# One gate before the last matrix product instead of a gate per chunk, and moved waits on the first casts of the q, k, v weights

## The chip, the cores and the metric

The kernel runs on the 8 cores of one Trainium2 chip, the same program on each. The metric is device time in microseconds (us) of the slowest core; lower is better. Each core has TensorE (PE, matrix products), VectorE (DVE), ScalarE (ACT), GpSimd (POOL) and SyncE (SP, here only a queue of transfers). Engines run their own instruction streams, in order, and wait for one another on semaphores.

## The reference, cut to what matters

One layer of a network on x of shape (4, 2048, 2048): a layer norm, linear attention with decay and rotary (16 heads of 128), a residual; a second layer norm, then a gated feed-forward part with a Walsh-Hadamard transform of the hidden vector, and a residual.

```python
    up_gate = jnp.einsum('bsd,hd->bsh', x, W1)        # h = 8192
    up_lin  = jnp.einsum('bsd,hd->bsh', x, W3)
    hidden  = jax.nn.silu(up_gate) * up_lin
    hidden  = fwht(hidden)                            # over all 8192 entries, / sqrt(8192)
    out     = jnp.einsum('bsh,dh->bsd', hidden, W2)
# fwht: h = 1, 2, 4, ..., 4096:  (a, b) -> (a + b, a - b) for entries h apart
...
    x = x + _L0_attn_ref(_layernorm(x), Wq, Wk, Wv, Wo, rms_w)
    x = x + _L0_ffn_ref(_layernorm(x), W1, W2, W3)
```

## The kernel before

Each core takes one half (T = 1024 tokens) of one of the four batch entries and does the whole layer for it, without talking to another core. Activations are kept as features on the 128 partitions by tokens along the free axis: x is 16 blocks of 128 by 1024.

The program is written as one list of instructions per engine, filled by `p.emit(engine, function, waits, inc)`; an engine runs its list in the order in which the Python code emits it. For DVE, ACT and POOL each instruction also waits for the one before it on its own engine and increments that engine's semaphore (`realize`). A wait that is already implied by an earlier wait of the same engine on the same semaphore is not emitted. `p.dma("sp", ...)` puts a transfer on SP's queue, `p.dma("act", ...)` on ACT's, `p.dma("pool", ...)` on POOL's; line 183 is the call that issues them.

The stages, in order of time: the state that the other half of the sequence hands over (L341 to L459); the first layer norm (`emit_layernorm`, L501 to L545, tag ln1), whose DVE part is 16 pairs of a subtraction (L543) and a product (L545) that writes `actA`; the q, k, v projections (L576 to L606); attention per head (L640 to L730); the RMS norm and the Wo product (L833, L843); the second layer norm; the feed-forward part.

**Projections.** For each of 48 weight slabs `gi`, SP loads a slab of 1 MB into `wland`, DVE casts it to bf16 in `wbf` (L587), PE does 32 products of 128x128 by 128x512 into `psumP` (L594), and ACT copies the result out (L603). Two buffers of each take turns. The cast waits for its load, for `ln1_done` (the last DVE instruction of the layer norm) and for the products that read the same buffer two slabs earlier.

**Hidden stage.** For 64 chunks of 128 hidden features, in bit-reversed order: 32 products with W1 (L926), 32 with W3 (L938), SiLU on ACT (L948), the product of the two on DVE (L951), one 128-point Hadamard step as a product with `H128s` (L957), and a copy into `hid` on ACT (L964). The other six levels of the transform join whole chunks: a butterfly on chunks (a, b) is a `tensor_add` (L973) and a `tensor_sub` (L976) on DVE, each 128x1024 bf16, written to free slots of `hid`. `fwht_schedule` emits after each chunk every butterfly that has become possible. After the last chunk, number 63, 63 butterflies are left, 126 DVE instructions. The first 31 finish the five lower levels of the odd chunks; the last 32 are the last level, on (0, 1), (2, 3), ..., (62, 63) in this order.

**Output stage.** out = W2 times hidden, in 4 blocks (`mblk`) of 512 output features. A block sums over all 64 chunks, in 16 groups of 4 chunks. For each group SP loads two halves of 512 KB of W2 into `land1`, ACT casts both into `wb1` (L1029), and PE does 32 products (L1045) into the four accumulators `p8`, which fill PSUM. There are two `wb1` and two `land1` buffers. At the end of a block DVE adds the residual that POOL loaded into `xpb` (L1060), and ACT's queue stores the four results, one after another; the casts of the next block stand behind these stores in ACT's list. The order of the groups, `cg_order`, is sorted by the number of the DVE instruction that finishes the group (`group_ready`), and each chunk's first product waits for the instruction that finished that chunk (`cgate`). Sorting leaves the groups in natural order 0, 1, ..., 15: by the schedule, groups 0 to 15 are finished by butterflies whose counts rise from 162 to 192 in steps of two.

Of the kernel before, what the change touches and what calls it, by code (L numbers as in the profile page):

```python
# [213 lines left out]
def build_program(taps=(), use_collective=True, upto="all"):  # L214
# [115 lines left out]
    for k in range(16):  # L330
        par = k % 2
# [246 lines left out]
    for widx, (wt, dst) in enumerate(((wq_h, q_hbm), (wk_h, k_hbm), (wv_h, v_hbm))):  # L578
        for m in range(16):
            gi = widx * 16 + m  # L580
            par = gi % 2
            p.dma("sp", wland[par][:, :], wt.ap()[m],
                  waits=[("dve", cast_val.get(gi - 2, p05_dve_end)),
                         ("pe", p05_pe_end if gi < 2 else 0),
                         ("act", s7_done if gi < 2 else 0)], inc=f"d_w{par}")
            cast_val[gi] = p.emit(
                "dve", lambda e, par=par: e.tensor_copy(wbf[par][:, :], wland[par][:, :]),  # L587
                waits=[(f"d_w{par}", 16 * (gi // 2 + 1)), ("dve", ln1_done),
                       ("pe", pe_proj.get(gi - 2, 0))], inc="dve")
            mm_waits = [("dve", cast_val[gi]), ("act", evac_val.get(gi - 2, 0))]  # L590
            pe_val = None
            for k in range(16):
                for half in range(2):
                    pe_val = p.emit("pe", lambda e, par=par, k=k, half=half: e.matmul(  # L594
                        psumP[par][:, half * 512:(half + 1) * 512],
                        wbf[par][:, k * 128:(k + 1) * 128],
                        actA[:, k * T + half * 512: k * T + (half + 1) * 512],
                        start=(k == 0), stop=(k == 15)),
                        waits=(mm_waits if (k == 0 and half == 0) else ()),
                        inc=("pe" if (k == 15 and half == 1) else None))  # L600
            pe_proj[gi] = pe_val
            evac_val[gi] = p.emit(
                "act", lambda e, par=par: e.activation(out=stg[par][:, :], in_=psumP[par][:, :],  # L603
                                                       func=AF.Copy),
                waits=[("pe", pe_val), (f"d_s{par}", 16 * store_val.get(gi - 2, 0))], inc="act")
            sv = p.dma("act", dst.ap()[m], stg[par][:, :], inc=f"d_s{par}")  # L606
            store_val[gi] = sv // 16
# [391 lines left out]
    blk_dve = {}  # L999
    p8_pe_val = {}  # L1000
    xb_pref = {}
    def group_ready(cg):
        vals = []
        for c in range(cg * 4, cg * 4 + 4):
            kind, val = chunk_src[c]
            vals.append(val if kind == "dve" else 0)
        return max(vals)
    cg_order = sorted(range(16), key=group_ready)
    for mblk in range(4):
        for m4 in range(4):  # L1010
            mchunk = mblk * 4 + m4
            p.dma("pool", xpb[m4][:, :], xp_hbm.ap()[mchunk],
                  waits=[("d_xp", 16 * xp_dma[15]),
                         ("pe", sa_pe_val[63] if mblk == 0 else 0),
                         ("dve", mul_val[63] if mblk == 0 else 0),
                         ("d_out", 16 * out_dma_val.get((mblk - 1, m4), 0))],
                  inc=f"d_xb{m4}")
            xb_pref[(mblk, m4)] = p.v(f"d_xb{m4}")
        for cgi in range(16):
            cg = cg_order[cgi]  # L1020
            par = cgi % 2
            gi = mblk * 16 + cgi
            for half in range(2):
                p.dma("sp", land1[half][:, :].rearrange("p (c m) -> p c m", c=2),
                      w2_h.ap()[mblk, cg * 4 + 2 * half: cg * 4 + 2 * half + 2].transpose([1, 0, 2]),
                      waits=[("act", w2cast.get((gi - 1, half), cast1_val[(63, half)] if gi == 0 else 0))],
                      inc=f"d_f1{half}")
            for half in range(2):
                w2cast[(gi, half)] = p.emit("act", lambda e, par=par, half=half: e.activation(  # L1029
                    out=wb1[par][:, half * 1024:(half + 1) * 1024], in_=land1[half][:, :],  # L1030
                    func=AF.Copy, scale=W2SCALE),
                    waits=[(f"d_f1{half}", 16 * (64 + gi + 1)),
                           ("pe", p8_pe_val.get(gi - 2, w13_pe_val[62 + par]))], inc="act")
            for cc in range(4):
                c = cg * 4 + cc
                hs = slot_of[c]
                ck, cv = chunk_src[c]
                cgate = cv if ck == "dve" else 0
                for m4 in range(4):
                    for half in range(2):  # L1040
                        st_ = (cgi == 0 and cc == 0)
                        sp_ = (cgi == 15 and cc == 3)
                        p8_pe_val[gi] = p.emit(
                            "pe", lambda e, par=par, cc=cc, m4=m4, half=half, hs=hs,
                                  st_=st_, sp_=sp_: e.matmul(  # L1045
                                p8[m4][:, half * 512:(half + 1) * 512],
                                wb1[par][:, cc * 512 + m4 * 128: cc * 512 + (m4 + 1) * 128],
                                hid[:, hs * T + half * 512: hs * T + (half + 1) * 512],
                                start=st_, stop=sp_),
                            waits=(([("act", w2cast[(gi, 1)])]  # L1050
                                    if (cc == 0 and m4 == 0 and half == 0) else []) +
                                   ([("dve", cgate)] if (m4 == 0 and half == 0) else []) +
                                   ([("dve", evac8.get((mblk - 1, m4), 0))]
                                    if (cc == 0 and half == 0 and cgi == 0) else [])),
                            inc=("pe" if (cc == 3 and m4 == 3 and half == 1) else None))
        blk_pe = p.v("pe")
        for m4 in range(4):
            mchunk = mblk * 4 + m4
            par = m4 % 2
            ev = p.emit("dve", lambda e, m4=m4: e.tensor_add(  # L1060
                xpb[m4][:, :], xpb[m4][:, :], p8[m4][:, :]),
                waits=[("pe", blk_pe), (f"d_xb{m4}", xb_pref[(mblk, m4)])], inc="dve")
            evac8[(mblk, m4)] = ev
            dv = p.dma("act", out_h.ap().rearrange("(k p) t -> p k t", p=128)[:, mchunk, :],
                       xpb[m4][:, :], waits=[("dve", ev)], inc="d_out")
            out_dma_val[(mblk, m4)] = dv // 16
        blk_dve[mblk] = p.v("dve")
# [49 lines left out]
```

How the kernel before makes its waits and increments, by code:

```python
            def f(e):  # L191
                selfsem = plan.sems.get(stream) if stream in plan.STRICT else None
                self_idx = 0
                for (waits, fn, sem, amt, is_self) in plan.ops[stream]:
                    for (s, v) in waits:
                        e.wait_ge(s, v)
                    if is_self and self_idx > 0:
                        e.wait_ge(selfsem, self_idx)
                    inst = fn(e)
                    if sem is not None:
                        inst.then_inc(sem, amt)
                    if is_self:
                        self_idx += 1
```

## Time and profile before

| what | us |
|---|---|
| time, median of 3 runs (range 3819.74 to 4116.42) | 3824.39 |
| the profiled execution, its own time | 3820.43 |
| its span on the slowest core, core 7 | 3818.8 |
| PE busy | 2571.3 (67%) |
| ACT busy | 1012.3 (27%) |
| DVE busy | 971.2 (25%) |

The span runs from the first to the last instruction on the core. A row of the profile's costliest groups reads: source line, engine and operation, output <- inputs, shape, count, then busy time, mean duration, and the idle time of that engine just ahead of it with what ended it. Durations of products overlap on PE (a product of 379 ns is followed by the next after some 216 ns), so busy time counts overlapped stretches once. PEclk is the clock that TensorE was granted, as a share of 2.4 GHz; 0.50 is the lower level, 1.2 GHz.

### The profile page before, as it was taken

The page shows a single profiled execution, that of the slowest core. Times are in us where ns is not written, and L with a number is a line of the kernel's source. Part 1 is how long each engine was busy: PE and PEld are TensorE (multiplying, and loading weights), DVE is VectorE, ACT ScalarE, POOL GpSimd, SP SyncE. Part 2 cuts the span into 40 slices and gives each one's busy share as a digit, 9 for nine tenths or more (in the row PEclk, how much of TensorE's full clock was granted, in tenths as well). Part 3 has the DMA queues.
Part 4 walks back from the last instruction along what each step waited for, and adds up shares of the span by engine and source line. Part 5 has one row for each costly group of instructions (what it writes and reads, how often), then busy time and mean ns, then how long its engine had stood idle before and what let it go on. Part 6 is the DMA issues. An engine that isn't in the chain of part 4 may idle for free.

```text
span 3818.8 us, 33708 instructions; the slowest of 8 cores (3802.6 to 3818.8 us)
## 1 busy us (share of the span) xinstructions
PE 2571.3 (67%) x11196; PEld 1088.7 (29%) x11196; DVE 971.2 (25%) x1312; ACT 1012.3 (27%) x1594; POOL 8.8 (0%) x20
## 2 busy tenths in 40 slices
PE   3355565576998222235478488788588788489888
PEld 0022222213443111111132133333233333134333
DVE  0412112114112444443320412221521221710000
ACT  1112122120111444431201233333233333123222
POOL 0000000000000000000000000000000000000000
PEclk9676776778999555557699699999799999799899
DMA  5422112113554011101141233333233343245453
GB/s 167 121 77 67 50 61 67 33 44 132 193 190 144 33 34 39 36 28 55 57 151 56 69 130 132 113 131 132 87 129 127 118 130 104 83 155 170 162 168 132
DMA packets 124218, 392.51 MB, mean 103 GB/s; under 512 B 12432, under 2 KB 12688, under 8 KB 115600
## 3 DMA queue, kind: packets, MB, share of 16 engines
q1 hardware_dynamic: 107920, 348.41, 27.5%
q10 hardware_dynamic: 13824, 33.56, 2.5%
q0 software_dynamic: 2304, 8.39, 0.7%
q8 instruction: 92, 1.51, 0.2%
q14 instruction: 78, 0.64, 0.1%
HBM read 356.76 MB, written 33.55 MB: 102 GB/s over the span
## 4 chain that ended last, share of the span: by engine, by line
PE 64%; DVE 17%; ACT 8%; issue 6%; DMA 4%; DVEq 1%; ACTq 1%; SPq 0%
PE p L1045 11%; PE pg L926 11%; PE pl L938 11%; PE psumP L594 9%; PE ppj L419 7%; PE psumW L833 3%; DVE htmp L951 2%; DVE hid L976 2%; DVE hid L973 2%; PE p_sx_ln L505 1%; PE p_sx_ln L511 1%; ACT ktp L452 1%; ACT ktil L694 1%; DVE actA L545 1%; DVE scrA L543 1%
## 5 line engine op out<-in xcount | busy, mean ns | idle before, releaser
L1045 PE MATMUL p<-hid,wb 128*128 128x512 bf16 x2048 | 451.5, 384 | 100.9 <-DVE hid L976 52.7
L926 PE MATMUL pg<-actA,wb 128*128 128x512 bf16 x2048 | 459.1, 383 | 43.0 <-DVE actA L545 43.0
L938 PE MATMUL pl<-actA,wb 128*128 128x512 bf16 x2048 | 452.5, 379 | 0.0
L594 PE MATMUL psumP<-actA,wbf 128*128 128x512 bf16 x1536 | 333.8, 381 | 44.4 <-DVE wbf L587 44.4
L419 PE MATMUL ppj<-xlnp,wbfp 128*128 128x512 bf16 x1024 | 259.5, 418 | 81.2 <-DVE wbfp L413 60.1
L1045 PEld LDWEIGHTS p<-hid,wb 128*128 128x128 bf16 x2048 | 201.9, 99 | 350.5 <-issue 115.2
L926 PEld LDWEIGHTS pg<-actA,wb 128*128 128x128 bf16 x2048 | 201.8, 99 | 292.2 <-issue 55.0
L938 PEld LDWEIGHTS pl<-actA,wb 128*128 128x128 bf16 x2048 | 200.4, 98 | 241.6
L951 DVE TENSOR_TENSOR htmp<-gsil,pl 128x1024 bf16<-128x1024 bf16 x64 | 78.1, 1221 | 745.4 <-PE pl L938 745.1
L1029 ACT ACTIVATE wb<-land 128x1024 bf16<-128x1024 f32 x128 | 135.2, 1056 | 404.6 <-PE p L1045 279.9
L964 ACT ACTIVATE hid<-pg 128x1024 bf16<-128x1024 f32 x64 | 65.5, 1024 | 580.5 <-PE pg L957 580.5
L594 PEld LDWEIGHTS psumP<-actA,wbf 128*128 128x128 bf16 x1536 | 150.7, 98 | 228.5 <-issue 48.7
L833 PE MATMUL psumW<-actA,wbf 128*128 128x512 bf16 x512 | 128.6, 415 | 86.7 <-DVE wbf L827 86.7
L705 PE MATMUL tp_O<-stil,vtok 128*128 128x128 bf16 x128 | 33.9, 265 | 208.1 <-ACT vtok L698 207.1
L419 PEld LDWEIGHTS ppj<-xlnp,wbfp 128*128 128x128 bf16 x1024 | 106.1, 106 | 229.1 <-issue 134.3
L973 DVE TENSOR_TENSOR hid<-hid 128x1024 bf16<-128x1024 bf16 x192 | 132.9, 692 | 88.9 <-ACT hid L964 70.5
L957 PE MATMUL pg<-htmp,H128s 128*128 128x512 bf16 x128 | 39.1, 387 | 166.2 <-DVE htmp L951 166.2
L913 ACT ACTIVATE wb<-land 128x1024 bf16<-128x1024 f32 x128 | 135.3, 1057 | 14.6 <-DMA land<-w_t 2.5
L910 ACT ACTIVATE wb<-land 128x1024 bf16<-128x1024 f32 x128 | 135.2, 1057 | 14.2 <-DMA land<-w_t 2.6
L603 ACT ACTIVATE stg<-psumP 128x1024 bf16<-128x1024 f32 x48 | 49.2, 1024 | 337.6 <-PE psumP L594 337.6
L976 DVE TENSOR_TENSOR hid<-hid 128x1024 bf16<-128x1024 bf16 x192 | 132.9, 692 | 20.3 <-DVE hid L973 0.5
L1060 DVE TENSOR_TENSOR xpb<-xpb,p 128x1024 f32<-128x1024 f32 x16 | 19.5, 1221 | 436.1 <-PE p L1045 434.9
(134 smaller groups left out, 2025.9 us busy)
## 6 DMA issues: line engine op xcount, KB each, us to landing
land<-w_t SPq DMA_DIRECT2D x384, 512.0 KB, 5.2
preland<-xp SPq DMA_DIRECT2D x32, 512.0 KB, 3.9
preland<-wk_t SPq DMA_DIRECT2D x32, 512.0 KB, 4.5
preland<-wv_t SPq DMA_DIRECT2D x32, 512.0 KB, 4.5
wland<-wq_t SPq DMA_DIRECT2D x16, 1024.0 KB, 5.2
wland<-wk_t SPq DMA_DIRECT2D x16, 1024.0 KB, 5.1
wland<-wv_t SPq DMA_DIRECT2D x16, 1024.0 KB, 5.2
wland<-wo_t SPq DMA_DIRECT2D x16, 1024.0 KB, 5.6
```

Source lines behind the costliest of these rows:

```text
L419: mmv = p.emit("pe", lambda e, k=k, half=half, wpar=wpar: e.matmul(ppj[:, half * 512:(half + 1) * 512], wbfp[wpar][:, k * 128:(k + 1) * 12 ...
L594: pe_val = p.emit("pe", lambda e, par=par, k=k, half=half: e.matmul(psumP[par][:, half * 512:(half + 1) * 512], wbf[par][:, k * 128:(k + 1 ...
L833: wo_pe = p.emit("pe", lambda e, par=par, k=k, half=half: e.matmul(psumW[par][:, half * 512:(half + 1) * 512], wbf[par][:, k * 128:(k + 1) ...
L910: cast1_val[(mi, half)] = p.emit("act", lambda e, par=par, half=half: e.activation(out=wb1[par][:, half * 1024:(half + 1) * 1024], in_=lan ...
L913: cast3_val[(mi, half)] = p.emit("act", lambda e, par=par, half=half: e.activation(out=wb3[par][:, half * 1024:(half + 1) * 1024], in_=lan ...
L926: w1_pe = p.emit("pe", lambda e, par=par, k=k, half=half: e.matmul(pg[par][:, half * 512:(half + 1) * 512], wb1[par][:, k * 128:(k + 1) * ...
L938: w13_pe = p.emit("pe", lambda e, par=par, k=k, half=half: e.matmul(pl[par][:, half * 512:(half + 1) * 512], wb3[par][:, k * 128:(k + 1) * ...
L951: mul_val[mi] = p.emit("dve", lambda e, par=par: e.tensor_mul(htmp[par][:, :], gsil[par][:, :], pl[par][:, :]), waits=[("act", silu_val[mi ...
L973: p.emit("dve", lambda e, fa=fa, sa_slot=sa_slot, sb_slot=sb_slot: e.tensor_add(hid[:, fa * T:(fa + 1) * T], hid[:, sa_slot * T:(sa_slot + ...
L976: last_bf = p.emit("dve", lambda e, fb=fb, sa_slot=sa_slot, sb_slot=sb_slot: e.tensor_sub(hid[:, fb * T:(fb + 1) * T], hid[:, sa_slot * T: ...
L1029: w2cast[(gi, half)] = p.emit("act", lambda e, par=par, half=half: e.activation(out=wb1[par][:, half * 1024:(half + 1) * 1024], in_=land1[ ...
L1045: st_=st_, sp_=sp_: e.matmul(p8[m4][:, half * 512:(half + 1) * 512], wb1[par][:, cc * 512 + m4 * 128: cc * 512 + (m4 + 1) * 128], hid[:, h ...
```

## The change

Two edits.

In the projections, the cast of a weight slab no longer waits for `ln1_done`; the first two casts wait for the ends of the stage before the layer norm on DVE, ACT and PE instead, and the first products of a slab wait for the later of their cast and `ln1_done`. The place of the casts in DVE's list is the same.

In the output stage, `group_ready`, `cg_order` and the wait per chunk go. Groups run in natural order, and the first product of each block waits for `last_bf`, the last instruction of the last butterfly.

```diff
             cast_val[gi] = p.emit(
                 "dve", lambda e, par=par: e.tensor_copy(wbf[par][:, :], wland[par][:, :]),
-                waits=[(f"d_w{par}", 16 * (gi // 2 + 1)), ("dve", ln1_done),
-                       ("pe", pe_proj.get(gi - 2, 0))], inc="dve")
-            mm_waits = [("dve", cast_val[gi]), ("act", evac_val.get(gi - 2, 0))]
+                waits=[(f"d_w{par}", 16 * (gi // 2 + 1)),
+                       ("dve", p05_dve_end if gi < 2 else 0),
+                       ("act", s7_done if gi < 2 else 0),
+                       ("pe", pe_proj.get(gi - 2, p05_pe_end))], inc="dve")
+            mm_waits = [("dve", max(cast_val[gi], ln1_done)), ("act", evac_val.get(gi - 2, 0))]
...
-    def group_ready(cg):
-        vals = []
-        for c in range(cg * 4, cg * 4 + 4):
-            kind, val = chunk_src[c]
-            vals.append(val if kind == "dve" else 0)
-        return max(vals)
-    cg_order = sorted(range(16), key=group_ready)
...
-        for cgi in range(16):
-            cg = cg_order[cgi]
-            par = cgi % 2
-            gi = mblk * 16 + cgi
+        for cg in range(16):
+            par = cg % 2
+            gi = mblk * 16 + cg
...
-                ck, cv = chunk_src[c]
-                cgate = cv if ck == "dve" else 0
...
-                        st_ = (cgi == 0 and cc == 0)
-                        sp_ = (cgi == 15 and cc == 3)
...
-                                start=st_, stop=sp_),
-                            waits=(([("act", w2cast[(gi, 1)])]
+                                start=(c == 0), stop=(c == 63)),
+                            waits=(([("act", w2cast[(gi, 1)]),
+                                     ("dve", last_bf if gi % 16 == 0 else 0)]
                                     if (cc == 0 and m4 == 0 and half == 0) else []) +
-                                   ([("dve", cgate)] if (m4 == 0 and half == 0) else []) +
                                    ([("dve", evac8.get((mblk - 1, m4), 0))]
-                                    if (cc == 0 and half == 0 and cgi == 0) else [])),
+                                    if (cc == 0 and half == 0 and gi % 16 == 0) else [])),
```

## Rows read from the trace of the kernel before

**Rows 1.** Spans and clocks: core, first to last instruction, mean granted TensorE clock
```profile
core 1: 3802.6 us, clock 0.831
...
core 7: 3818.8 us, clock 0.829
```

**Rows 2.** Costliest groups of the page: busy, mean ns | idle before, releaser
```profile
L1045 PE MATMUL p<-hid,wb 128*128 128x512 bf16 x2048 | 451.5, 384 | 100.9 <-DVE hid L976 52.7
L926 PE MATMUL pg<-actA,wb 128*128 128x512 bf16 x2048 | 459.1, 383 | 43.0 <-DVE actA L545 43.0
L594 PE MATMUL psumP<-actA,wbf 128*128 128x512 bf16 x1536 | 333.8, 381 | 44.4 <-DVE wbf L587 44.4
```

**Rows 3.** Waits after 3240 us: who waited for whom: total us, times, longest
```profile
PE p L1045 <- DVE hid L976: 52.7, 1, 52.7
PE p L1045 <- ACT wb L1029: 48.3, 5, 17.7
```

**Rows 4.** Timeline of DVE around the 126 last butterfly instructions: start, duration
```profile
3254.88 0.69 DVE L973 TENSOR_TENSOR hid<-hid 128x1024 bf16<-128x1024 bf16 x1 [2.20 <-ACT hid L964]
...
3305.36 0.69 DVE L976 TENSOR_TENSOR hid<-hid 128x1024 bf16<-128x1024 bf16 x1
3306.16 0.69 DVE L973 TENSOR_TENSOR hid<-hid 128x1024 bf16<-128x1024 bf16 x1
...
3355.06 0.69 DVE L976 TENSOR_TENSOR hid<-hid 128x1024 bf16<-128x1024 bf16 x1
```

**Rows 5.** L976 alone in two stretches: DVE busy (x count), PEclk, DMA share, GB/s
```profile
3254.80:3306.10 51.30, 22.14 (x32) 0.51 0.23 82
3306.10:3356.00 49.90, 21.46 (x31) 0.95 0.37 125
```

**Rows 6.** Timeline of PE at the start of the output stage
```profile
3306.20 112.88 PE L1045 MATMUL p<-hid,wb 128*128 128x512 bf16 x512 [52.67 <-DVE hid L976]
```

**Rows 7.** Timeline of PE, the three later blocks of the output stage
```profile
3433.88 8.60 PE L1045 MATMUL p<-hid,wb 128*128 128x512 bf16 x32 [14.79 <-ACT wb L1029]
3443.04 103.76 PE L1045 MATMUL p<-hid,wb 128*128 128x512 bf16 x480 [0.57 <-ACT wb L1029]
3564.50 113.43 PE L1045 MATMUL p<-hid,wb 128*128 128x512 bf16 x512 [17.70 <-ACT wb L1029]
3692.34 9.07 PE L1045 MATMUL p<-hid,wb 128*128 128x512 bf16 x32 [14.41 <-ACT wb L1029]
3702.21 103.76 PE L1045 MATMUL p<-hid,wb 128*128 128x512 bf16 x480 [0.80 <-ACT wb L1029]
```

**Rows 8.** Timeline of ACT, casts of W2 around PE's start
```profile
3254.80 2.21 ACT L1029 ACTIVATE wb<-land 128x1024 bf16<-128x1024 f32 x2
3264.87 2.21 ACT L1029 ACTIVATE wb<-land 128x1024 bf16<-128x1024 f32 x2 [7.86 <-DMA land<-w_t]
3315.64 2.21 ACT L1029 ACTIVATE wb<-land 128x1024 bf16<-128x1024 f32 x2 [48.56 <-PE p L1045]
3322.54 2.21 ACT L1029 ACTIVATE wb<-land 128x1024 bf16<-128x1024 f32 x2 [4.70 <-PE p L1045]
```

**Rows 9.** Stretches, core 7: length, busy PE, PEld, DVE, ACT, POOL, PEclk, DMA, GB/s
```profile
3306.00:3312.00 6.00, 5.80 (x17) 2.19 (x18) 5.17 (x9) 0.00 (x0) 0.00 (x0) 0.61 0.01 3
3312.00:3406.00 94.00, 94.00 (x438) 42.58 (x436) 37.80 (x55) 28.05 (x27) 0.00 (x0) 1.00 0.44 146
```

**Rows 10.** The same view, one stretch on cores 3 and 4, one of each die
```profile
3356.00:3406.00 50.00, 50.00 (x234) 22.67 (x232) 0.00 (x0) 12.67 (x12) 0.00 (x0) 1.00 0.43 144
...
3356.00:3406.00 50.00, 50.00 (x233) 22.64 (x232) 0.00 (x0) 14.80 (x14) 0.00 (x0) 1.00 0.50 157
```

**Rows 11.** Timeline of DVE and PE where the first projections start
```profile
886.97 1.22 DVE L545 TENSOR_TENSOR actA<-scrA,p_br_ln 128x1024 bf16<-128x1024 f32 x1
888.37 2.56 DVE L587 CAST wbf<-wland 128x2048 bf16<-128x2048 f32 x2 [0.17 <-DVE actA L545]
...
889.74 15.45 PE L594 MATMUL psumP<-actA,wbf 128*128 128x512 bf16 x61 [44.37 <-DVE wbf L587]
```

More of the change, by code:

```diff
@@ L1036, in build_program @@
                 hs = slot_of[c]
-                ck, cv = chunk_src[c]
-                cgate = cv if ck == "dve" else 0
                 for m4 in range(4):
                     for half in range(2):
-                        st_ = (cgi == 0 and cc == 0)
-                        sp_ = (cgi == 15 and cc == 3)
                         p8_pe_val[gi] = p.emit(
-                            "pe", lambda e, par=par, cc=cc, m4=m4, half=half, hs=hs,
-                                  st_=st_, sp_=sp_: e.matmul(
+                            "pe", lambda e, par=par, cc=cc, m4=m4, half=half, hs=hs, c=c: e.matmul(
                                 p8[m4][:, half * 512:(half + 1) * 512],
```

## The prediction, made before the changed kernel was run

> **What bounds the kernel now.** I read the page first, its table of busy time and its costliest groups. PE carries the span with 67% busy, and its big groups are the products of the hidden, projection and output stages; the group rows also say how long PE stood idle ahead of each and who ended that [rows 2]. Two of these idle times touch the diff: 44.4 us ahead of the projections, ended by the cast at L587, and 100.9 us around the output stage, of which 52.7 us were ended by a butterfly at L976. The spans of the cores come next: they lie between 3802.6 and 3818.8 us, at mean clocks of 0.831 and 0.829, so no core is a special case and core 7 can be read for all [rows 1].
>
> Then the waits of the last 580 us. PE's waits there are one of 52.7 us for a butterfly and five for a cast of W2, 48.3 us together [rows 3]. The timelines say what the first is. After chunk 63 of the hidden stage DVE starts the 126 instructions of the last 63 butterflies at 3254.88 us, one every 0.80 us [rows 4]. PE starts the output stage at 3306.20 us [rows 6], long before DVE is done: the last L976 starts at 3355.06 us [rows 4]. The instruction that releases PE can be named. Chunk 0 is finished by the 32nd butterfly of the tail (31 that finish lower levels, then (0, 1)), which is the tail's 64th instruction and the 32nd at L976. In the stretch up to 3306.1 us there are 32 of L976, and 31 after it [rows 5]; the 32nd starts at 3305.36 us and ends 0.69 us later, at 3306.05 us, and PE follows 0.15 us behind [rows 4, 6].
>
> From there the 512 products of block 0 run without a hole in 112.88 us [rows 6]. They need two chunks every 16 products, 3.45 us at the rate of 480 in 103.76 us [rows 7], while DVE finishes two chunks in two instructions, 1.6 us. So after the first chunk no gate ever holds PE: the per-chunk gate lets PE overlap all of the last 62 DVE instructions. Every microsecond from PE's start to the end is chain: block, edge between blocks, block.
>
> **The change, part by part.**
>
> *The casts of the first two projection slabs.* The wait on `ln1_done` goes, but the casts keep their place in DVE's list, behind the 32 instructions of the layer norm. DVE runs its list in order, and each instruction waits for its predecessor anyhow. In the trace the first cast starts at 888.37 us, 0.17 us behind the end of the last L545, and PE starts 0.14 us after it ends (two casts in 2.56 us) [rows 11]. Without the wait it can't start earlier, since what stands ahead of it is not the semaphore but 32 instructions. The new waits name things that ended before the layer norm began. The products' new wait, the later of cast and `ln1_done`, is the cast, as before. From above, one more wait instruction costs no more than that whole gap of 0.17 us; from below, if the cast did leave the path, 1.28 us plus the gap, 1.5 us, would be saved. I take 0, nearest to the row, since the order is fixed.
>
> *The order of groups.* The sort gave the natural order, so PE's list, the weights' list and the start and stop flags are the same. Cost 0; nothing is hidden by it that could come out.
>
> *The gate.* The first product of block 0 now waits for the tail's 126th instruction instead of its 64th. That is 62 instructions more, and in the trace the two start at 3305.36 and 3355.06 us: 49.70 us apart [rows 4]. The lag to PE stays at 0.15 us. PE's start moves from 3306.20 to 3355.90 us.
>
> Does the tail itself change when PE no longer works beside it? The 63 intervals ahead of PE's start take 3305.36 - 3254.88 = 50.48 us, 0.801 us each, and the 62 beside it 49.70 us, 0.802 us each [rows 4]. PE beside DVE costs nothing, so its absence gives at most 0.1 us.
>
> *The removed gates in block 0.* Up to 32 waits in PE's list go. Block 0, with them, takes 112.88 us, and block 2, without any, 113.43 us [rows 6, 7]. What they cost is below what separates two blocks, so 0; from below I keep 0.6 us as what could be saved.
>
> *What stands behind the waiting PE.* Behind PE's first product stand all other products; who waits for them is ACT (the cast for the third group needs its `wb1` buffer), SP behind ACT (the loads need `land1`), and at the block's end DVE and the stores. ACT cast the first two groups at 3254.80 and 3264.87 us and then waited 48.56 us for PE's first group; from there it follows PE, one pair of casts per 6.9 us [rows 8]. After the change it waits 49.7 us longer in the same place. Two buffers are full either way, so the longer wait lets nothing run ahead. POOL's first four loads of the residual wait for the end of the hidden stage and not for this gate.
>
> *What is late next.* Everything from PE's start on, by the same 49.70 us on each core: four blocks and the three edges between them. Block plus edge took 127.7, 131.1 and 128.0 us for blocks 1 to 3 (from the end of block 0 at 3419.08 us to the end of each) [rows 6, 7]. The edges hold stores, loads of the residual and the reload of W2 on shared transfer engines, so they can fall out a little differently: all three at 127.7 us would give back 3.7 us, all at 131.1 us would cost 6.5 us.
>
> *TensorE's clock.* PE restarts cold after its idle time: in the first 6 us of block 0 the granted clock averages 0.61, between 1.2 and 2.4 GHz, and then it is 1.00 [rows 9]. Block 0, after 52.67 us idle, takes 112.88 us; block 2, after 17.70 us idle, takes 113.43 us [rows 6, 7]. Three times the idle time did not make the restart dearer, so doubling it from 52.7 to 102.4 us should not either. I take 0, with 0.6 us to either side.
>
> *Sum.* 3820.43 (own time of the profiled execution) + 0 + 0 + 49.70 + 0 = 3870.1 us. The median of the runs shown lies 4 us above that execution's time, and the lowest 0.7 us below it; I put the forecast at 3871 us, +1.3%. Two percent of this kernel are 76 us, about what a measurement of it can tell from no change, so the forecast is a loss inside of that band.
>
> **The rivals.**
>
> *The clock is lower after the restart (slower by over 2%).* All cores end a longer idle time and start the dense stage at 1.2 GHz. A block whose 512 products all ran at 1.2 GHz would take twice 103.76 x 512/480 = 110.7 us, so the forecast would become 3871 + 110.7 = 3982 us. It leaves the 2% band when PE spends another 53 us at 1.2 GHz, since half of it is lost and 26.7 us are missing to 76.4. For it: the restart is cold [rows 9]. Against it: block 0 already follows 52.67 us of idle and is at 1.00 after 6 us [rows 6, 9], and a core of each die holds 1.00 in the dense middle of that block [rows 10]. Chance 0.04.
>
> There is a rule of the Trainium skill for such a loss, in the page "TensorE: Matmul & The Clock Gate", section "Part 1: The HAM clock gate", in its note on the peak-current limiter: once a third core of a die starts dense products, the whole die goes to 13/16 of the full clock for as long as the load lasts. By that rule this kernel, with four dense cores a die, would run its 451.5 us of output products [rows 2] 16/13 as long, 104 us more, before the change as well as after it; if it struck only after the change, the time would be 3975 us. The trace disagrees: 1.00 on all of the cores read. The sum goes by the trace.
>
> *The delay is paid back at the edges (not slower).* With 50 us more before PE starts, W2 would be far enough ahead that the edges between blocks vanish. Blocks 1 to 3 and their edges take 386.9 us and three bare blocks 3 x 110.7 = 332.1 us, so 54.8 us are there to be had, and 3870.1 - 54.8 = 3815 us would be the time. It decides the sign only if over 49.7 of the 54.8 us go. For it: PE waits 48.3 us for casts of W2 [rows 3]. Against it: the two-buffer limit above, seen as ACT's wait of 48.56 us for PE [rows 8], and the order of ACT's list, in which the next block's casts stand behind the stores of the last. Chance 0.03.
>
> *The gate does not bite (no change, 3820 us).* This would be so if PE had been held to the end of the butterflies already, or by W2. The rows exclude the first, with PE running from 3306.20 us beside DVE [rows 4, 6], and the second, with two groups cast by 3267 us [rows 8]. Chance 0.02.
>
> *The gate's own price is doubled (3920 us).* A second event of the size of the shift, at a block edge, where a core's stores and loads meet those of others in another phase. All cores are shifted by the same 62 instructions, so their phases to each other stay; an edge's largest excess in the trace is 3.4 us. It needs more than 26 us to pass the band. Chance 0.02.
>
> **How the numbers follow.** Forecast 0.89, the rivals 0.04, 0.03, 0.02, 0.02. The range around 3871: below, 3.7 us from the edges, 1.5 from the cast, 0.6 from the gates, 0.6 from the clock and 1 from the standing of the execution, 7.4 together, and 4.7 for how whole runs of one kernel differ (3819.74 against 3824.39): 3871 - 12.1 = 3859. Above, 6.5 + 0.2 + 0.6 and 3 for the median, 10.3 together, and the same 4.7: 3871 + 15 = 3886. This holds the likeliest case and leaves out the rivals. Faster by over 2%: none of the cases gives it, 0.01 for what I did not see. Slower by over 2%: clock and doubled price, 0.06. Within 2%: 0.93.
>
> **What would show it.** In the changed kernel's profile: PE's one wait for L976 before L1045 grows from 52.7 to 102.4 us; PE's first L1045 comes 0.15 us after the end of the last L976, not of the 32nd; DVE's tail keeps 0.80 us per instruction and has no product beside it; ACT's wait for PE before the third pair of casts is near 98 us; block 0 keeps 113 us and blocks with edges 128 to 131 us; the first cast still stands 0.2 us behind the last L545, with PE's wait at 44.4 us. I would be wrong by the clock if the granted clock in block 0 stayed below 1.00 after its first 6 us, by the edges if their waits for casts left 48 us by more than 10, and by the whole reading if PE's first product of the output stage still came at 3306 us.

## The result, and the profile after

| | before | after |
|---|---|---|
| profiled execution, us | 3820.43 | 3867.85 |
| its span on the slowest core | 3818.8 (core 7) | 3866.3 (core 2) |
| lowest of all runs | 3819.74 | 3867.85 |
| PE's wait for the butterflies ahead of the output stage | 52.7 | 102.4 |

The change costs 1.4%: the ratio of the times is 1.014, with a 95% interval from 1.0122 to 1.0157. The median of the 9 runs after, 3884.79 us, lies higher than that ratio says, because some executions of either kernel have a die with a lower granted clock, and the ratios in this text leave those out.

The costliest groups of the page after the change (line, engine, operation, busy, mean ns, idle before and what ended it) answer to [rows 2]; the lines have moved, L1045 is now L1034, L926 is L928, L594 is L596.

```profile
L1034 PE MATMUL p<-hid,wb 128*128 128x512 bf16 x2048 | 450.4, 383 | 155.3 <-DVE hid L978 102.4
L928 PE MATMUL pg<-actA,wb 128*128 128x512 bf16 x2048 | 459.0, 383 | 43.0 <-DVE actA L545 43.0
L940 PE MATMUL pl<-actA,wb 128*128 128x512 bf16 x2048 | 452.5, 379 | 0.0
L596 PE MATMUL psumP<-actA,wbf 128*128 128x512 bf16 x1536 | 333.8, 381 | 44.3 <-DVE wbf L587 44.3
```

Only one of them has a different idle time: the output stage, 155.3 us where it was 100.9, and the part that a butterfly ended went from 52.7 to 102.4 us. The projections still wait 44.3 us for the cast at L587. The waits of the last 620 us say the same, with the wait for casts of W2 beside it [rows 3]:

```profile
PE p L1034 <- DVE hid L978: 102.4, 1, 102.4
...
PE p L1034 <- ACT wb L1023: 52.9, 5, 16.9
```

The timelines of DVE and PE around the gate, core 2. The first row is the first instruction of the tail, the second the last:

```profile
3249.31 0.69 DVE L975 TENSOR_TENSOR hid<-hid 128x1024 bf16<-128x1024 bf16 x1 [2.19 <-ACT hid L966]
...
3349.52 0.69 DVE L978 TENSOR_TENSOR hid<-hid 128x1024 bf16<-128x1024 bf16 x1
```

```profile
3350.36 112.03 PE L1034 MATMUL p<-hid,wb 128*128 128x512 bf16 x512 [102.39 <-DVE hid L978]
3478.68 9.11 PE L1034 MATMUL p<-hid,wb 128*128 128x512 bf16 x32 [16.29 <-ACT wb L1023]
3489.25 103.76 PE L1034 MATMUL p<-hid,wb 128*128 128x512 bf16 x480 [1.46 <-ACT wb L1023]
3609.86 8.38 PE L1034 MATMUL p<-hid,wb 128*128 128x512 bf16 x32 [16.85 <-ACT wb L1023]
3620.59 103.76 PE L1034 MATMUL p<-hid,wb 128*128 128x512 bf16 x480 [2.34 <-ACT wb L1023]
3740.28 113.32 PE L1034 MATMUL p<-hid,wb 128*128 128x512 bf16 x512 [15.93 <-ACT wb L1023]
```

The reader is to see three things. The tail is as long as before: from its first start to its last 100.21 us, against 100.18 us [rows 4]. PE begins 0.15 us after the last L978 has ended, where before it began 0.15 us after the 32nd. And the blocks behind it look much as they did: block 0 with 112.03 us, then edges of some 16 us and blocks of 113.3 to 114.5 us, their short inner waits counted, where before they took 112.9 to 113.6 us [rows 7].

The difference of the two profiled executions, 47.42 us, can be laid out from these rows. The wait brings 102.39 - 52.67 = 49.7 us. From PE's start to the end of its last block it is 503.2 us, where it was 499.8 us [rows 6, 7], 3.4 us more: block 0 is 0.9 us shorter, the rest with its edges 4.3 us longer. The hidden stage ended 5.6 us earlier than in the profiled execution before, the last Hadamard product starting at 3247.37 us on core 2 against 3252.94 us on core 7. 49.7 + 3.4 - 5.6 is 47.5 us. The 5.6 us are not the change's: the cores of one execution of the kernel before start that product anywhere from 3241.14 to 3253.89 us.

### The profile page after: what moved, and what is told of

It reads as the page before. It is cut to its first block, busy times and chain, and to the rows that moved or that the text cites. A ratio compares the mean times of both kernels' runs of the same rounds, so it can differ in the third digit from the quotient of the medians.

```text
span 3866.3 us, 33677 instructions; the slowest of 8 cores (3858.6 to 3866.3 us)
## 1 busy us (share of the span) xinstructions
PE 2567.7 (66%) x11196; PEld 1087.2 (28%) x11196; DVE 971.3 (25%) x1312; ACT 1011.7 (26%) x1594; POOL 8.8 (0%) x20
## 4 chain that ended last, share of the span: by engine, by line
PE 63%; DVE 18%; ACT 8%; issue 6%; DMA 4%; DVEq 1%; ACTq 1%; SPq 0%
PE p L1034 11%; PE pg L928 11%; PE pl L940 11%; PE psumP L596 9%; PE ppj L419 7%; PE psumW L835 3%; DVE hid L978 2%; DVE hid L975 2%; DVE htmp L953 2%; PE p_sx_ln L505 1%; PE p_sx_ln L511 1%; ACT ktp L452 1%; ACT ktil L696 1%; DVE actA L545 1%; DVE scrA L543 1%
## 5 line engine op out<-in xcount | busy, mean ns | idle before, releaser
L1034 PE MATMUL p<-hid,wb 128*128 128x512 bf16 x2048 | 450.4, 383 | 155.3 <-DVE hid L978 102.4
L928 PE MATMUL pg<-actA,wb 128*128 128x512 bf16 x2048 | 459.0, 383 | 43.0 <-DVE actA L545 43.0
L596 PE MATMUL psumP<-actA,wbf 128*128 128x512 bf16 x1536 | 333.8, 381 | 44.3 <-DVE wbf L587 44.3
L1034 PEld LDWEIGHTS p<-hid,wb 128*128 128x128 bf16 x2048 | 201.7, 99 | 403.9 <-issue 168.0
L928 PEld LDWEIGHTS pg<-actA,wb 128*128 128x128 bf16 x2048 | 201.8, 99 | 292.1 <-issue 54.9
L596 PEld LDWEIGHTS psumP<-actA,wbf 128*128 128x128 bf16 x1536 | 150.8, 98 | 228.5 <-issue 48.8
L978 DVE TENSOR_TENSOR hid<-hid 128x1024 bf16<-128x1024 bf16 x192 | 132.9, 692 | 20.3 <-DVE hid L975 0.5
```

Source lines behind the costliest of these rows:

```text
L928: w1_pe = p.emit("pe", lambda e, par=par, k=k, half=half: e.matmul(pg[par][:, half * 512:(half + 1) * 512], wb1[par][:, k * 128:(k + 1) * ...
L978: last_bf = p.emit("dve", lambda e, fb=fb, sa_slot=sa_slot, sb_slot=sb_slot: e.tensor_sub(hid[:, fb * T:(fb + 1) * T], hid[:, sa_slot * T: ...
L1034: "pe", lambda e, par=par, cc=cc, m4=m4, half=half, hs=hs, c=c: e.matmul(p8[m4][:, half * 512:(half + 1) * 512], wb1[par][:, cc * 512 + m4 ...
```

## The experiments

Each is the kernel before, or the changed kernel where it says so, with the edit shown. Ratios are to the kernel before on the same chip.

### The gate without the casts, and the casts without the gate

The theory was that the gate is the whole of the cost, 49.7 us. The rival was that the moved waits in the projections carry a part. The first kernel has the gate and the old waits of the casts:

```diff
             # the changed kernel
-                       ("dve", p05_dve_end if gi < 2 else 0),
-                       ("act", s7_done if gi < 2 else 0),
-                       ("pe", pe_proj.get(gi - 2, p05_pe_end))], inc="dve")
-            mm_waits = [("dve", max(cast_val[gi], ln1_done)), ("act", evac_val.get(gi - 2, 0))]
+                       ("dve", ln1_done), ("pe", pe_proj.get(gi - 2, 0))], inc="dve")
+            mm_waits = [("dve", cast_val[gi]), ("act", evac_val.get(gi - 2, 0))]
```

> The changed kernel with its first edit undone: the casts of the projection weights wait for ln1_done again, the single gate on last_bf stays. Theory (the gate is the whole cost): the span is 49.7 us above the kernel before, near 3870 us, ratio 1.013, PE's wait for the last butterfly 102.4 us. Rival (the waits of the casts or of the products in the projections carry part of the 1.4%): less than that, by as much as the run with the casts alone lies above 1.

The second is the kernel before with exactly the opposite edit, the new waits of the casts alone.

> The kernel before with the first edit alone: the casts no longer wait for ln1_done. Theory: no change, 3820 to 3824 us, ratio 1.000 within 0.3%; the first cast still starts within 0.3 us of the end of the layer norm's last product on DVE, and PE waits 44.4 us. Rival: the casts leave the path (1.5 us less) or the longer waits cost something (4 us or more, what the ratio of the change has above 49.7 us).

Measured: the gate alone gives a ratio of 1.0101 (1.0046 to 1.0156), its profiled execution 3872.55 us, PE's wait 102.4 us. The casts alone give 0.9979 (0.9942 to 1.0016) and a median of 3822.57 us, against 3821.89 us for the kernel before in the same job, both over the executions that the ratios count. The waits of PE, first of the gate alone, then of the casts alone. The last line of each is the wait ahead of the projections:

```profile
PE p L1032 <- DVE hid L976: 102.4, 1, 102.4
PE p L1032 <- ACT wb L1021: 48.6, 5, 15.3
...
PE psumP L594 <- DVE wbf L587: 44.4, 1, 44.4
```

```profile
PE p L1047 <- DVE hid L978: 52.7, 1, 52.7
PE p L1047 <- ACT wb L1031: 47.6, 4, 16.0
...
PE psumP L596 <- DVE wbf L587: 44.3, 1, 44.3
```

Both intervals are wide, and by themselves they would leave room for 21 and for 14 us on either side. The waits do not: all 49.7 us sit in the gate, and the casts' edit leaves the wait for the butterfly at 52.7 us and the wait ahead of the projections at 44.3 us, within 0.1 us of what it was [rows 11]. DVE's timeline of the kernel with the casts alone shows why. Without the wait the cast begins 0.10 us behind the end of the last product of the layer norm, where with it it was 0.17 us [rows 11]:

```profile
888.79 1.22 DVE L545 TENSOR_TENSOR actA<-scrA,p_br_ln 128x1024 bf16<-128x1024 f32 x1
890.11 2.56 DVE L587 CAST wbf<-wland 128x2048 bf16<-128x2048 f32 x2
```

### The casts moved for real

Was it the place in DVE's list that held the casts? Here the loads and casts of slabs 0 and 1 are emitted inside of the layer norm, behind its statistics and ahead of its 32 normalizing instructions:

```diff
+        if early is not None:
+            early()          # loads of slabs 0 and 1, and their casts to wbf
         ctx2 = ExitStack()
         p_bm = ctx2.enter_context(nc.psum_tensor(f"p_bm_{tag}", [128, T], F32))
```

> The kernel before with the first two casts of the projections really moved: they are emitted ahead of the layer norm's 32 normalizing DVE instructions, where DVE waits for ScalarE and TensorE, with their loads. Theory (what held them was their place in DVE's list, not the wait): PE's wait ahead of the projections falls from 44.4 to 43.0 us, the time by 1.4 us, not to be told apart in the ratio. Rival (the wait held them): no difference to the kernel with the waits alone changed, 44.4 us.

Measured: ratio 0.9991 (0.9981 to 1.0001). The timelines of DVE, then PE:

```profile
837.06 2.56 DVE L574 CAST wbf<-wland 128x2048 bf16<-128x2048 f32 x2
...
887.96 1.22 DVE L547 TENSOR_TENSOR actA<-scrA,p_br_ln 128x1024 bf16<-128x1024 f32 x1
```

```profile
889.33 16.05 PE L607 MATMUL psumP<-actA,wbf 128*128 128x512 bf16 x61 [42.62 <-DVE actA L547]
```

The two casts now run at 837.06 us, in a hole of DVE, and PE is released by the last product of the layer norm itself. Its wait falls from 44.37 to 42.62 us, 1.75 us where 1.4 were expected. Of these, 1.40 us lie behind the end of the last L547: PE starts 0.15 us after it, where before it started 1.55 us after the last L545 [rows 11]. The other 0.35 us lie ahead of that end and are not explained. So the wait could be shortened, by the place of the casts and not by their semaphores; it is worth little more than the 1.28 us that one cast lasts, below what the ratio can tell.

### A gate in the middle, and a gate further back

If the price is the number of DVE instructions waited for, it must grow in a straight line with the place of the gate. In the first kernel only the very first product waits for the tail's 95th instruction:

```diff
                 cgate = cv if ck == "dve" else 0
+                if cgi == 0 and cc == 0:
+                    cgate = max(cgate, last_bf - 31)
```

> The kernel before, in which only the first product of the output stage waits for the 95th instruction of DVE's tail instead of its 64th; all gates per chunk stay. Theory (price = number of DVE instructions waited for in addition x 0.80 us): 31 x 0.80 = 24.9 us, ratio 1.0065, PE's wait 77.5 us. Rival (cost comes from the form of the gate, or the two streams disturb each other when they overlap): it does not lie halfway, but near 0 or near 50 us.

In the second, the changed kernel gets 62 more DVE instructions behind the tail, and waits for the last of them:

```diff
+    for i in range(62):
+        last_bf = p.emit("dve", lambda e: e.tensor_add(
+            hid[:, free_slots[0] * T:(free_slots[0] + 1) * T],
+            hid[:, slot_of[0] * T:(slot_of[0] + 1) * T],
+            hid[:, slot_of[1] * T:(slot_of[1] + 1) * T]), inc="dve")
```

> The changed kernel with 62 more DVE instructions of the same size behind the tail, whose results nobody reads, and the gate on the last of them. Theory (a linear price, and a restart of PE that does not depend on how long it stood idle): another 49.6 us, PE's wait 152 us, block 0 between 112 and 114 us, 3820.4 + 99.3 = 3920 us, ratio 1.026. Rival (a longer idle time makes the restart dearer, or the clock low): block 0 above 116 us, ratio above 1.03.

Measured: 1.0062 (1.0047 to 1.0077) and 1.0257 (1.0232 to 1.0281). PE's first block in each, the middle gate (core 2, with a mean granted clock of 0.98 over this block), then the later one (core 4):

```profile
3408.18 112.44 PE L1047 MATMUL p<-hid,wb 128*128 128x512 bf16 x502 [77.69 <-DVE hid L973]
```

```profile
3401.24 112.69 PE L1039 MATMUL p<-hid,wb 128*128 128x512 bf16 x502 [152.06 <-DVE hid L987]
```

With the gate at the tail's 64th, 95th, 126th and 188th instruction PE waits 52.67, 77.69, 102.39 and 152.06 us: 25.0, 49.7 and 99.4 us more for 31, 62 and 124 instructions, 0.80 us each. The ratios follow, 0.6%, 1.4% and 2.6%. Block 0 takes 112.9, 112.4, 112.0 and 112.7 us behind these waits, so a longer idle time does not make the restart dearer. DVE keeps 0.80 us for each instruction with products beside it and without, and the length of block 0 does not follow the overlap: it is 112.4 us with 31 butterfly instructions beside it, and 112.0 and 112.7 us with none. Both rivals, a dearer restart and a disturbance between the streams, fall.

### The tail in the order of demand

If only the instruction that finishes chunk 0 counts, the tail can be ordered so that it comes early. The 63 butterflies stay the same (the function is printed in a shortened form):

```diff
-    return sched
+    return sched[:63] + [demand_order(sched[63])]
+
+def demand_order(pairs):      # each butterfly just ahead of the first chunk, 0..63, that needs it
+    out, done = [], set()
+    def need(i):
+        if i in done: return
+        a, b = pairs[i]
+        for j in range(i):
+            if set(pairs[j]) & {a, b}: need(j)
+        done.add(i)
+        out.append(pairs[i])
+    for c in range(64):
+        for i, pr in enumerate(pairs):
+            if c in pr: need(i)
+    return out
```

Chunk 0 now needs six butterflies: (31, 63), (15, 31), (7, 15), (3, 7), (1, 3), (0, 1).

> The kernel before with the 63 last butterflies in another order, each just ahead of the first chunk that needs it; the work is the same. Chunk 0 is then finished by the tail's 12th instruction. Theory: PE starts 52 instructions earlier, 52 x 0.80 = 41.5 us, and is not held afterwards since it takes 1.73 us per chunk against DVE's 1.6: PE's first wait 11.2 us, ratio 0.989, near 3780 us. Rival (PE and DVE share something, or PE catches up with DVE): PE waits more times for L976, the gain is below 30 us.

The same order in the changed kernel, with its single gate:

> The changed kernel with the last 63 butterflies in the order of demand, as in the run before it. Theory (only the count of DVE instructions ahead of PE's first product matters): with one gate the order of the tail is worth nothing, the time is that of the changed kernel, +49.7 us, ratio 1.013, PE's wait 102.4 us; the single gate costs 91 us against the same order with gates per chunk. Rival (a better order helps the tail itself): it lies below the changed kernel by 5 us or more.

Measured: 3780.58 us as the median of four runs that lie within 2.8 us, against 3821.89 us, over the executions that the ratios count, so 41.3 us less where 41.5 were expected. The ratio is 0.9846, but its interval is wide (0.9747 to 0.9946) and gives the size only roughly; what fixes it is PE's wait, 41.73 us shorter than before. With the single gate the ratio is 1.0124 (1.0101 to 1.0147). Their first blocks, gates per chunk first, then the single gate (core 2):

```profile
3264.26 113.36 PE L1065 MATMUL p<-hid,wb 128*128 128x512 bf16 x512 [10.94 <-DVE hid L996]
```

```profile
3353.36 112.02 PE L1054 MATMUL p<-hid,wb 128*128 128x512 bf16 x502 [102.36 <-DVE hid L998]
```

PE waits once for a butterfly, 10.94 us, and then runs through 512 products while DVE finishes the other chunks ahead of it, by 2 to 18 us if each chunk takes PE 1.73 us and each instruction DVE 0.80 us (an estimate from these rows). With the single gate the wait is 102.36 us, and the better order is worth nothing: its ratio agrees with the 1.014 of the changed kernel. The price of the gate is thus not a property of the gate: it is the distance between the first chunk's instruction and the last one, 49.7 us in one order and 91.4 us in the other.

### A version that beats both

The same reading shows a second place where PE waits for DVE: in the hidden stage the Hadamard product of each chunk waits for the product at L951, in the kernel before 64 times, 166.2 us together, once 38.7 us. The long ones are butterflies queued ahead of it on DVE, the short ones the 1.65 us that DVE takes. In the kernel before:

```profile
PE pg L957 <- DVE htmp L951: 166.2, 64, 38.7
```

Two edits on top of the order of demand: at most 8 butterflies are emitted behind a chunk, and the Hadamard product of a chunk is emitted behind the W1 products of the next.

```diff
-        for (a, b) in sched[mi]:
+        backlog.extend(sched[mi])
+        now = list(backlog) if mi == 63 else backlog[:8]
+        del backlog[:len(now)]
+        for (a, b) in now:
...
         # PE's list for chunk mi: W1 products, then
+        if mi > 0: finish_pe(mi - 1)      # the Hadamard product of the chunk before
         # then W3 products; copy and butterflies of chunk mi - 1 stand behind the DVE product of mi
```

The version with both edits was run first, and the version with the first edit alone, and the one with the single gate, after its time of 3601 us was known.

> The part of the fast version without its moved Hadamard product: order of demand in the tail, and at most 8 butterflies behind each chunk of the hidden stage. Theory: PE's waits for L951 fall from 166 us in total, 64 times and 38.7 us at most, to 64 times 1.65 us, 106 us, so 60 us go on top of the 41.5 us: 3820 - 101 = 3719 us, ratio 0.973. What is left to the fast version at 3601 us is then the price of the Hadamard product's place, near 118 us. Rival (spreading helps little, the place of the Hadamard product carries all): 3770 us or more.

> A version meant to beat both: order of demand in the tail; at most 8 butterflies behind each chunk of the hidden stage instead of up to 31; and the Hadamard product of a chunk behind the W1 products of the next chunk, so that PE does not wait for the product on DVE. Theory: 41.5 us from the tail, and nearly all of the 166 us that PE waits for L951 in the hidden stage: 3820 - 41 - 160 = 3620 us, ratio 0.948. Rival (ACT's casts and copies or the loads of W1 and W3 become the bound, at about 14 us a chunk): a gain of 41 us and less than half of the 166 us, above 3700 us.

> The fast version with one added wait: the first product of the output stage waits for the last butterfly, as in the changed kernel. Theory (the gate's price is the count of DVE instructions between the first chunk's and the last butterfly, here 126 - 12 = 114): 114 x 0.80 = 91 us, 3601 + 91 = 3692 us, ratio 0.966 to the kernel before, PE's wait 102.4 us. Rival (in a kernel that is fuller on PE, the rest given to PE is partly paid back, by the clock or by the edges of blocks): under 80 us.

Measured: the first edit with the order of demand 0.9722 (0.9693 to 0.975), median 3713.93 us; both edits 0.9415 (0.9398 to 0.9432), median 3600.59 us; both, with the single gate, 0.9661 (0.9633 to 0.9689), median 3692.07 us, the medians again over the executions that the ratios count. PE's waits ahead of the Hadamard product with the first edit:

```profile
PE pg L978 <- DVE htmp L972: 106.6, 64, 2.1
```

and the last waits of PE with both edits, then with the single gate added:

```profile
PE p L1084 <- ACT wb L1068: 46.9, 3, 15.8
PE p L1084 <- DVE hid L970: 10.9, 1, 10.9
...
PE pg L943 <- DVE htmp L1015: 1.7, 1, 1.7
```

```profile
PE p L1086 <- DVE hid L970: 102.4, 1, 102.4
```

Spreading leaves 64 waits of at most 2.1 us, and moving the product leaves one of 1.7 us. Spreading alone came out 5 us below the 3719 us expected, so its rival, that spreading helps little, falls. Moving the product as well took off another 113 us, where near 118 were expected. The version with both edits takes 5.9% less time than the kernel before. It was expected at 0.948, near 3620 us, and came out at 0.9415, some 19 us lower. The first line of its page (busy time of each engine) shows most of that difference:

```profile
PE 2555.5 (71%) x11196; PEld 1092.3 (30%) x11196; DVE 970.9 (27%) x1312; ACT 1012.3 (28%) x1594; POOL 8.8 (0%) x20
```

PE's waits for DVE in the hidden stage fell by 164.5 us where the expectation took 160, and PE's busy time, which it took as fixed, fell from 2571.3 to 2555.5 us, by 15.8 us. Of these, 5.3 us are the W1 products (459.1 to 453.8 us). The rest was not tried; an estimate from the rows is 64 stops fewer, each of which had left the end of a product uncovered, 379 - 216 ns, 10.4 us together.

In this version the single gate costs 3692.07 - 3600.59 = 91.5 us, where 114 instructions of 0.80 us gave 91: nothing is paid back in a fuller kernel.

## Why the prediction was right, point by point

**The gate.** 62 instructions, 49.70 us: PE's wait grew by 49.72 us. The reading that made this sum possible was which instruction released PE, the 32nd L976; the four places of the gate confirm 0.80 us for each instruction.

**The casts.** Taken as 0, bounded by 1.5 us: nothing in the time, PE's wait 44.30 us against 44.37. The bound held for what it was made of, one cast and the gap: with the casts really moved, 1.40 us went there, and another 0.35 us ahead of it that the prediction did not see.

**The order of groups and the removed gates.** Both 0. Block 0 without its gates takes 112.03 us, 0.85 us less than with them, a little more than the 0.6 us allowed. That the gates are not the reason is seen in two other runs: with the gates kept it took 112.44 us behind the middle gate, without them 112.69 us behind the later one. The difference lies in the restart (see the clock).

**What is late next.** Everything behind PE's start moved. ACT's wait for PE ahead of its third pair of casts was put near 98 us and is 96.00 us. The second pair of casts was 1.4 us later after the tail's start than before, since its load landed later, and PE freed the first buffer 0.9 us sooner; the length of that wait has no bearing on the end.

**The edges.** Blocks 1 to 3 with their edges take 391.2 us on core 2, 4.3 us more than the 386.9 us on core 7 before, inside of the bounds of -3.7 and +6.5 us. PE's waits for casts of W2 went from 48.3 to 52.9 us; with the gate alone they are 48.6 us. Core 2 is the longest of the eight here: over all cores the same stretch takes 384.7 to 391.2 us, mean 387.0, after, and 382.4 to 388.4 us, mean 385.8, before. So most of the 4.3 us is scatter between cores. Whether the 1.2 us between the means belong to the change is not shown. Nothing was paid back.

**The clock.** The restart is no dearer after 102.4 us idle than after 52.7. In the first 6 us, taken from 0.2 us ahead of PE's start as in [rows 9], the granted clock averages 0.75, where before it was 0.61, and then it is 1.00:

```profile
3350.16:3356.16 6.00, 5.80 (x21) 2.42 (x22) 0.05 (x1) 0.00 (x0) 0.00 (x0) 0.75 0.01 3
...
3360.00:3462.00 102.00, 102.00 (x474) 46.20 (x473) 0.00 (x0) 28.53 (x27) 0.00 (x0) 1.00 0.44 145
```

The 0.14 more, over 6 us, make up the 0.85 us by which block 0 is shorter on this core. It is not so on every core: six of the eight took 112.0 us, and cores 0 and 4 took 113.6 us after the same 102.39 us idle. The forecast took 0 here, with 0.6 us to either side; that was right in size and a little narrow.

**The total.** 3871 us was forecast, 1.3%; the ratio gives 1.4%, and 1.3% lies inside of its interval. The range of 3859 to 3886 us took in the median of all runs, 3884.79 us, but only just, and that is partly luck: the forecast was made for the likeliest case, and this median lies 17 us above the lowest run, for the reason given with the result. What bears the forecast out is the ratio and the profiled execution, 3867.85 us. That execution in turn comes within 3 us of the sum, 3870.1 us, partly because two things that the sum left at 0 nearly cancel, 5.6 us less ahead of the tail and 3.4 us more behind PE's start. The prediction was right for its reasons: the one term of its sum is the one that was measured.

## What to carry to other kernels

When a wait is made coarser, its price is not the length of the work it waits for. It is the distance, on the producer, between the instruction that used to release the consumer and the one that does now, as long as the consumer then never catches up. Count the instructions between the two and take their interval from the trace. The same distance is what can be won: order the producer's work by what the consumer needs first. A wait taken from an instruction that stands right behind others on its own in-order engine changed nothing here (44.37 and 44.30 us); to start it earlier, it has to stand earlier in the list.

## What the runs showed of the hardware

The price of TensorE's restart does not grow with the time that it stood idle, from 11 us on. The 512 products of block 0 took 113.4, 112.9, 112.4, 112.0 and 112.7 us after idle times of 10.9, 52.7, 77.7, 102.4 and 152.1 us, against 110.7 us at the rate of 480 products in 103.76 us. That is a loss of 1.3 to 2.7 us, and 2.9 us on cores 0 and 4 of the changed kernel. The granted clock in the first 6 us tells the same: 0.53, 0.61, 0.68, 0.75 and 0.64, in the same order. What makes one restart a microsecond dearer than another was not tried. The Trainium skill, "TensorE: Matmul & The Clock Gate", section "Part 1: The HAM clock gate", describes this as a clock gate with two levels, which activity releases. The runs agree: while PE waits for the butterflies the granted clock is 0.51 [rows 5], and after the first 6 us of products it is 1.00 [rows 9].

The prediction set aside that section's note on a peak-current limiter, since the trace of before showed 1.00. A level near the one that the note gives, 13/16, does appear in another trace. In the profiled execution of the single gate with the order of demand, cores 4 and 5 were granted 0.81 through the dense middle of the output stage, while core 2, on the other die, had 1.00. Core 5, then core 2:

```profile
3380.00:3500.00 120.00, 120.00 (x458) 49.71 (x457) 0.00 (x0) 29.59 (x28) 0.00 (x0) 0.81 0.36 123
```

```profile
3380.00:3450.00 70.00, 69.63 (x319) 31.74 (x325) 0.00 (x0) 21.12 (x20) 0.00 (x0) 1.00 0.46 156
```

Core 5's block 0 took 135.85 us, core 2's 112.02 us, a ratio of 1.21, close to the page's 16/13. But cores 6 and 7, on the same die as core 5, did not share it: their block 0 took 112.03 and 112.01 us. Core 6:

```profile
3427.28 112.03 PE L1054 MATMUL p<-hid,wb 128*128 128x512 bf16 x512 [102.36 <-DVE hid L998]
```

In the projections of the same execution it was the other way round: from 950 to 1150 us of its own time core 6 was granted 0.81, and core 5 1.00; core 5 did not hold 0.81 in a dense stretch until 3150 us. Each core's time counts from its own start; for these two stretches to be one event, the starts would have to lie some 2000 us apart in an execution of 3970.76 us. So the level is seen here, but by these rows not for a whole die at once, as the note has it. Nor is it seen whenever three cores of a die run dense products: in the trace of the kernel before, all eight cores had 1.00 in the middle of block 0. What sets it off was not tried.
